# Weighted rows of an attention layer as two float32r parts, a ring of 10 groups instead of 12, and a later change of the scatter lag

## The reference

```
# first layer: an MLP on each edge, its mean at the source node
h = concat([x[src], x[dst]]);  h = tanh(h @ W0 + b0);  h = tanh(h @ W1 + b1)
h = (h @ W2 + b2) * (edge_attr @ Wg)
x = layernorm(x + segment_mean(h, src))
# second layer: attention with 4 heads of 64
h = einsum('ni,hio->hno', x, W);  e = leaky(attn_src[src] + attn_dst[dst]) * edge_weight
alpha = exp(e - max(e)) / segment_sum(exp(e - max(e)), dst)
x = layernorm(x + segment_sum(h[src] * alpha, dst))
```

## Time and profile before

| | us |
|---|---|
| median of 3 runs | 2397.0 |
| lowest and highest | 2392.29, 2398.76 |
| profiled execution | 2396.2 |
| its span, first to last instruction | 2394.1 |

### The profile page before, as it was taken

How to read it: one execution, slowest core, us unless ns; L and a number is a source line. 1 busy time by engine, 2 the same in 40 slices (tenths; PEclk the granted TensorE clock), 3 DMA queues, 4 the chain that set the end, 5 groups by cost and what they waited for, 6 DMA issues and landing times. The chain is left out here.

```text
span 2394.1 us, 38204 instructions
## 1 busy us (share of the span) xinstructions
PE 1902.2 (79%) x12132; PEld 1623.5 (68%) x12132; DVE 1426.5 (60%) x4037; ACT 1211.2 (51%) x2298; POOL 1522.9 (64%) x1253
## 2 busy tenths in 40 slices
PE   7799999989999999999999999954245555455560
PEld 7688888878888888888888888843133444333350
DVE  6556666656666666666666666653165455454475
ACT  2477777757777777777777777734000000000012
POOL 0427777777787777777777777734655565555513
PEclk9899999999999999999999999977566676766685
DMA  7798877777777777777777887674344444444423
GB/s 247 253 237 198 179 169 163 153 152 157 163 163 161 161 165 160 164 163 162 163 162 169 175 177 174 134 198 122 97 110 121 120 131 118 119 114 122 114 80 110
DMA packets 239706, 370.92 MB, mean 155 GB/s; under 512 B 33255, under 2 KB 172481, under 8 KB 239495
## 3 DMA queue, kind: packets, MB, share of 16 engines
q0 software_dynamic: 104688, 191.38, 40.5%
q1 hardware_dynamic: 134807, 177.00, 25.0%
HBM read 260.28 MB, written 107.97 MB: 154 GB/s over the span
## 5 line engine op out<-in xcount | busy, mean ns | idle before, releaser
L1549 POOL DMA_INDIRECT accA<-ystage,to_a x391 | 639.3, 1635 | 204.7 <-issue 105.7
L1555 POOL DMA_INDIRECT GA<-TA,src_c x391 | 436.5, 1116 | 246.0 <-issue 108.5
L1606 POOL DMA_INDIRECT Hg<-HT,src_c x391 | 376.2, 962 | 266.9 <-DVE xb L1118 152.0
L644 DVE TENSOR_TENSOR h2l<-h2f,h2h 128x512 fp32r<-128x512 f32 (+1 forms) x294 | 203.2, 691 | 307.3 <-ACT h2h L1997 159.9
L1681 PE MATMUL bank<-h1h,W1h 128*128 128x512 f32 x882 | 355.1, 403 | 12.9 <-DVE h1l L644 12.9
L1682 PE MATMUL bank<-h1l,W1h 128*128 128x512 f32 x882 | 349.0, 396 | 0.0
L1683 PE MATMUL bank<-h1h,W1l 128*128 128x512 f32 x882 | 348.8, 395 | 0.0
L2034 ACT ACTIVATE h1f<-bank 128x512 f32<-128x512 f32 (+1 forms) x392 | 220.7, 591 | 243.0 <-PE bank L1736 196.8
L1926 PE MATMUL bank<-xb,in_window 128*128 128x260 f32 (+1 forms) x782 | 277.3, 501 | 62.5 <-issue 60.7
L2177 ACT ACTIVATE drop<-neg_m 128x1 f32<-128x1 f32 x49 | 14.4, 295 | 548.9 <-DVE neg_m L1113 376.5
L1926 PEld LDWEIGHTS bank<-xb,in_window 128*128 128x128 f32 (+1 forms) x782 | 187.9, 252 | 112.7 <-issue 82.2
(11 more groups left out here) (252 smaller groups left out, 4498.3 us busy)
## 6 DMA issues: line engine op xcount, KB each, us to landing
ef<-in_eT SPq DMA_DIRECT2D x97, 256.0 KB
bcast_i<-in_src_row SPq DMA_DIRECT2D x97, 256.0 KB
TW<-TB SPq DMA_DIRECT2D x116, 203.0 KB
HB<-hist SPq DMA_DIRECT2D x98, 130.0 KB
rel<-RL SPq DMA_DIRECT2D x97, 128.0 KB
rem<-RD SPq DMA_DIRECT2D x48, 256.0 KB
TB<-stB SPq DMA_DIRECT2D x24, 406.0 KB
accA<-zeros SPq DMA_DIRECT2D x4, 2193.0 KB, 15.6
```

The source lines that it names most:

```text
L644: return dve.tensor_tensor(o, full, hi.bitcast(f32), ALU.subtract)
L1549: return pool.indirect_dma_start(out=table, out_offset=bass.IndirectOffsetOnAxis(ap=rows, axis=0), in_=sums, in_offset=None, compute_op=AL ...
L1555: pool.indirect_dma_start(out=GA[0:n, b % (GAR * BLOCKS_PER_GROUP), :].bitcast(f32), out_offset=None, in_=TA, in_offset=bass.IndirectOffse ...
L1606: pool.indirect_dma_start(out=Hg[0:n, slot, :], out_offset=None, in_=HT, in_offset=bass.IndirectOffsetOnAxis(ap=src_c[0:n, b:b + 1], axis= ...
```

## The change

It does five things.

1. `SLOW_START` goes from 20 to 91: `lag` is 3 for groups 0 to 90.
2. `HGR` goes from 12 to 10, and `chosen`, used after the last pair, lies in slots of `Hg`.
3. `xb` becomes a plain float32 ring of 2 groups without the weights' columns. ACT copies it into `xb_hi` (float32r, 4 groups; new `upper_rows`), whose last 4 columns are the exponentials; DVE subtracts `xb_hi` from `xb` into `xb_lo` (float32r, 2 groups; new `lower_rows`), once a group, and once a pair the 4 weight columns. `in_window` becomes float32r.
4. `window_sums` does two float32r products a block, one with `xb_hi` and one with `xb_lo`, and waits for `s_xb_lo` rather than `s_xb`.
5. The semaphores `s_pad` and `s_mg` are merged into `s_zero` and `s_nm`, with the counts changed to suit; the other branch gets a buffer of its own, `xb_u`.

`lower_rows(2q)` stands on DVE after `weighted_rows(2q + 1)`, and `lower_rows(2q + 1)` after `edge_scores(q + 2)`, ahead of `one_hot(q + 3)`. `same_rows` splits a list of blocks into those with 128 rows and the last, shorter one; `lo(o, full, hi)` is a DVE subtraction.

```diff
-SLOW_START = 20
+SLOW_START = 91
...
-        chosen = sb("chosen", [P, NT, NG], f32, sc)
...
-        HGR = 12
+        HGR = 10
...
+        chosen = Hg[:, 2 * BLOCKS_PER_GROUP:HGR * BLOCKS_PER_GROUP, :].rearrange("p b d -> p (b d)")[:, 0:NT * NG]\
+            .rearrange("p (t g) -> p t g", g=NG)
...
-        xb = sb("xb", [P, XBR * BLOCKS_PER_GROUP, BW], f32, s2)
-        in_window = sb("in_window", [P, XBR * BLOCKS_PER_GROUP, P], f32, s2)
+        xb = sb("xb", [P, 2 * BLOCKS_PER_GROUP, OUT], f32, s2)
+        xb_hi = sb("xb_hi", [P, XBR * BLOCKS_PER_GROUP, BW], f32r, s2)
+        xb_lo = sb("xb_lo", [P, 2 * BLOCKS_PER_GROUP, BW], f32r, s2)
+        xb_u = sb("xb_u", [P, BW], f32, s2)
+        in_window = sb("in_window", [P, XBR * BLOCKS_PER_GROUP, P], f32r, s2)
...
             def weighted_rows(g):
 
                 dve.wait_ge(s_ex, g // 2 + 1)
+                if g >= 2:
+                    dve.wait_ge(s_xb_lo, g - 1)
+                for run in same_rows(blocks_of_group(g)):
+                    n, b, k = rows_of_block(run[0]), run[0], len(run)
+                    i, r = b % (2 * BLOCKS_PER_GROUP), b % (HGR * BLOCKS_PER_GROUP)
+                    last = weigh(xb[0:n, i:i + k, :], Hg[0:n, r:r + k, 0:OUT], weight_p(g // 2)[0:n, i:i + k], n, k)
+                last.then_inc(s_xb, 1)
+
+            def lower_rows(g):
+
+                if g % 2 == 0:
+                    dve.wait_ge(s_S, g)
+                    for run in same_rows(blocks_of_window_pair(g // 2)):
+                        n, b, k = rows_of_block(run[0]), run[0], len(run)
+                        j, i = b % (XBR * BLOCKS_PER_GROUP), b % (2 * BLOCKS_PER_GROUP)
+                        lo(xb_lo[0:n, i:i + k, OUT:BW], weight_p(g // 2)[0:n, i:i + k], xb_hi[0:n, j:j + k, OUT:BW])
+                dve.wait_ge(s_xb_hi, g + 1)
                 for run in same_rows(blocks_of_group(g)):
                     n, b, k = rows_of_block(run[0]), run[0], len(run)
                     j, i = b % (XBR * BLOCKS_PER_GROUP), b % (2 * BLOCKS_PER_GROUP)
-                    r = b % (HGR * BLOCKS_PER_GROUP)
-                    last = weigh(xb[0:n, j:j + k, 0:OUT], Hg[0:n, r:r + k, 0:OUT], weight_p(g // 2)[0:n, i:i + k], n, k)
-                last.then_inc(s_xb, 1)
+                    last = lo(xb_lo[0:n, i:i + k, 0:OUT], xb[0:n, i:i + k, :], xb_hi[0:n, j:j + k, 0:OUT])
+                last.then_inc(s_xb_lo, 1)
 
             def carry_window(g):
 
...
                     weighted_rows(2 * q + 1)
+                    lower_rows(2 * q)
                 if 0 <= q - 1:
...
                     edge_scores(q + 2)
+                if 0 <= q < NQ:
+                    lower_rows(2 * q + 1)
                 if q + 3 < NQ:
...
             def window_sums(g):
 
                 pe.wait_ge(s_win, g // 2 + 1)
-                pe.wait_ge(s_xb, g + 1)
+                pe.wait_ge(s_xb_lo, g + 1)
                 if g >= 3:
                     pe.wait_ge(s_carry, g - 2)
                 blocks = blocks_of_group(g)
                 for b in blocks:
                     n, j = rows_of_block(b), b % (XBR * BLOCKS_PER_GROUP)
-                    last = pe.matmul(PS[g % 3][:, 0:BW], in_window[0:n, j, :], xb[0:n, j, :],
-                                     start=b == blocks[0], stop=b == blocks[-1])
+                    pe.matmul(PS[g % 3][:, 0:BW], in_window[0:n, j, :], xb_hi[0:n, j, :], start=b == blocks[0], stop=False)
+                    last = pe.matmul(PS[g % 3][:, 0:BW], in_window[0:n, j, :], xb_lo[0:n, b % (2 * BLOCKS_PER_GROUP), :],
+                                     start=False, stop=b == blocks[-1])
                 last.then_inc(s_S, 1)
 
             pe.wait_ge(s_hc, NT)
...
 
 
             act.wait_ge(s_dc, DC["no maximum"])
-            for q in range(NQ):
-                act.wait_ge(s_nm, q + 1)
+            def exponentials(q):
+
+                act.wait_ge(s_nm, 2 * (q + 1))
                 act.activation(drop[:, q:q + 1], neg_m[:, q:q + 1], ACT.Exp, bias=neg_m[:, q + 1:q + 2], scale=-1.0)\
                     .then_inc(s_drop, 1)
                 if q >= 2:
...
                     j, i = b % (XBR * BLOCKS_PER_GROUP), b % (2 * BLOCKS_PER_GROUP)
                     act.activation(weight_p(q)[0:n, i:i + k], score[0:n, b:b + k, :], ACT.Exp,
                                    bias=neg_m[0:n, q + 1:q + 2])
-                    last = act.activation(xb[0:n, j:j + k, OUT:BW], score[0:n, b:b + k, :], ACT.Exp,
+                    last = act.activation(xb_hi[0:n, j:j + k, OUT:BW], score[0:n, b:b + k, :], ACT.Exp,
                                           bias=neg_m[0:n, q + 1:q + 2])
                 last.then_inc(s_ex, 1)
+
+            def upper_rows(g):
+
+                act.wait_ge(s_xb, g + 1)
+                if g >= XBR:
+                    act.wait_ge(s_S, g - XBR + 1)
+                for run in same_rows(blocks_of_group(g)):
+                    n, b, k = rows_of_block(run[0]), run[0], len(run)
+                    j, i = b % (XBR * BLOCKS_PER_GROUP), b % (2 * BLOCKS_PER_GROUP)
+                    last = copy(xb_hi[0:n, j:j + k, 0:OUT], xb[0:n, i:i + k, :])
+                last.then_inc(s_xb_hi, 1)
+
+            exponentials(0)
+            for q in range(NQ):
+                upper_rows(2 * q)
+                if q + 1 < NQ:
+                    exponentials(q + 1)
+                upper_rows(2 * q + 1)
             for i in range(2):
                 last = act.activation(factor[:, :].rearrange("p (q i) -> p q i", i=2)[:, :, i], neg_m[:, 1:NQ + 1], ACT.Exp,
                                       bias=neg_m[:, NQ:NQ + 1], scale=-1.0)
```

More of the change, by code:

```diff
@@ L492, in build_program @@
         s_sp = sem("s_sp")
-        s_mg = sem("s_mg")
         s_nm = sem("s_nm")
@@ L499, in build_program @@
         s_xb = sem("s_xb")
+        s_xb_hi = sem("s_xb_hi")
+        s_xb_lo = sem("s_xb_lo")
         s_S = sem("s_S")
@@ L1107, in running_maximum @@
                 if q >= 2:
[L1108 to L1112, removed]
+                    dve.wait_ge(s_nm, 2 * (q - 1))
+                dve.tensor_reduce(top_g[:, q % 2:q % 2 + 1], PTOP[:, 0:P], AX.X, ALU.max).then_inc(s_nm, 1)
+                dve.wait_ge(s_nm, 2 * q + 1)
                 dve.scalar_tensor_tensor(neg_m[:, q + 1:q + 2], top_g[:, q % 2:q % 2 + 1], -1.0, neg_m[:, q:q + 1],
@@ L1288, in _ @@
                     dve.wait_ge(s_vg, 64 * NB + 16 * (b + 1))
-                    step(dve.tensor_copy(xb[0:n, 0, OUT:BW], score[0:n, b, :]))
-                    step(weigh(xb[0:n, 0:1, 0:OUT], Hg[0:n, 0:1, 0:OUT], score[0:n, b:b + 1, :], n, 1), ("weighed", b))
+                    step(dve.tensor_copy(xb_u[0:n, OUT:BW], score[0:n, b, :]))
+                    step(weigh(xb_u[0:n, 0:OUT].unsqueeze(1), Hg[0:n, 0:1, 0:OUT], score[0:n, b:b + 1, :], n, 1), ("weighed", b))
             def attention_residual(c):
@@ L1358, in _ @@
             sp.dma_start(TB[N:N + P, :].rearrange("p (k d) -> p k d", k=4),
-                         zeros[:, 0:H0 // 2].unsqueeze(1).to_broadcast([P, 4, H0 // 2])).then_inc(s_pad, 16)
+                         zeros[:, 0:H0 // 2].unsqueeze(1).to_broadcast([P, 4, H0 // 2])).then_inc(s_zero, 16)
             sp.wait_ge(s_dc, DC["rem"])
@@ L1428, in _ @@
                         sp.wait_ge(s_tb[k], stores(N0R, k))
-                    sp.wait_ge(s_pad, 16)
+                    sp.wait_ge(s_zero, 16)
                 if g + 2 < NG:
@@ L1580, in _ @@
                 if 0 in added:
-                    pool.wait_ge(s_zero, 32 * TABLES)
+                    pool.wait_ge(s_zero, 16 + 32 * TABLES)
                 for j in range(BLOCKS_PER_GROUP):
@@ L1913, in spread_maxima @@
                 if q >= 1:
-                    pe.wait_ge(s_mg, q)
+                    pe.wait_ge(s_nm, 2 * q - 1)
                 pe.matmul(PTOP[:, 0:P], ones[:, :], diag[:, q % 2, :], start=True, stop=True).then_inc(s_sp, 1)
@@ L1980, in _ @@
                         pe.wait_ge(s_vact, VACT1 + 1 + b)
-                    pe.matmul(bank[0][0:n, 0:BW], in_window[0:n, 0, 0:n], xb[0:n, 0, :],
+                    pe.matmul(bank[0][0:n, 0:BW], in_window[0:n, 0, 0:n].bitcast(f32), xb_u[0:n, :],
                               start=True, stop=True).then_inc(s_vpe, 1)
```

1 line of the change is left out of this document (removed).

## The result

The changed kernel takes 2371.6 us in the median of 5 runs (2358.39 to 2381.24) against 2397.82 for the kernel before: ratio 0.9881, 95% interval 0.985 to 0.9913. It is 26 us faster where 25 us slower was forecast. The forecast had POOL's waits for `xb` at 180 to 190 us and the remote wait near 200; they came out at 93.1 and 116.6. The profiled execution has a span of 2356.3 us and a mean TensorE clock of 0.849.

A forecast was written before the change was run, and what follows sets the result against it. It took PE to bound most of the first layer, and POOL's gathers, pausing for credits while PE's results came late, the second. Terms 26 + 4 - 2 + 6 - 8 = +26 us gave 2422; own range 2402 to 2458, overall 2300 to 2462.

The forecast's parts named there:

- A rule against the change: Second layer: DVE subtractions with two SBUF inputs contend with POOL's gathers; +10 us for 3 of 16, +60 for all.
- rival C: Second layer: subtractions beside gather runs cost +89 us at most, 2511, or give 2432 to 2482; 0.14 together with Rival B.
- Step 1: Second layer, split on DVE and ACT: odd group's subtraction lengthens POOL's pause from 7.1 to 8.4 us; +26 (0 to +55).
- Step 2: Second layer, ring of 10 groups: 48 instead of 56 gathers run free; +4 us (0 to 8.4), 2 taken off.
- Step 3: Second layer after the last gather: one pair less in the ring, five pairs pay 2.63 us each; +6 (0 to 13).
- Step 4: Second layer's window products: float32r makes them shorter, but nobody waits for PE's work, only for its results; 0.
- rival A: Second layer: float32r brings PE's results sooner, the remote wait goes; 2246 in full (chance 0.11), 2331 in part (0.21).
- Step 6: First layer, the longer lag: PE's loss at 458 to 551 goes, SP's tile wait returns later; -8 us (-19 to +5).
- Rival B: Second layer: late credits cut POOL's runs to 12 gathers; 2481, or 2451 with only the even subtraction; 0.14 with rival C.
- Rival D: Whole kernel: the lag's full -19 us pays for the split at half price; 2398, no change; chance 0.09.

The follow-up runs named there:

- lower_psum: Changed kernel with DVE's large subtraction replaced by an equally long product with one PSUM input, PE multiplying xb_hi twice: 2420.62 against 2390.54 us, ratio 1.0105.
- split_f32_2: Changed kernel with one float32 product of xb_hi a block, xb_lo made but not multiplied, on a chip holding results back: 2388.29 us, ratio 0.9992.
- ring10: Kernel before with HGR 10 instead of 12 and nothing else, on a chip not holding results back: 2201.02 us, ratio 0.9997.
- upper_only: Changed kernel without lower_rows: DVE subtracts nothing, PE multiplies xb_hi twice; results held back: 2382.28 us, ratio 0.9975.
- after_lag20: Changed kernel with SLOW_START back at 20, on a chip not holding results back: 2226.44 us, ratio 1.0095 to the kernel before.
- lag_only: Kernel before with only SLOW_START changed from 20 to 91, on a chip not holding results back: 2198.75 against 2204.75 us, ratio 0.9978.
- type_only_2: Kernel before with two float32r products a block, both of the same rows, no split; results held back: 2398.29 us, ratio 1.0048.
- after_paced3: Changed kernel with POOL also waiting for L1906 of the pair 3 before; results not held back: 2215.5 against 2203.58 us, ratio 1.0058.
- few_ad: Kernel before with one instead of three products per block in destination_scores; results not held back: 2204.29 us, ratio 1.0002.
- Paced: Kernel before with SLOW_START 91 and POOL waiting before each pair's gathers for PE's L1906 of the pair 4 before: 2317.2 us, ratio 0.9696.
- paced3: Kernel before with SLOW_START 91 and POOL waiting for PE's L1906 of the pair 3 before: 2313.0 us, ratio 0.9667; repeated, 2314.85 us, 0.9703.
- gap: Kernel before with SLOW_START 91 and a 0.43 us POOL copy once in every four gathers: 2351.72 us, ratio 0.9815.

## Why the prediction was wrong

*The step that failed* is the one on the port ("A rule against the change"), with its rival C. The sum has no term for the port, and C priced the stall of a gather beside a subtraction as a cost only, +10 to +89. Its size is now seen: the gathers took 24.8 us more in all (1.026 for 0.962 in the mean). The +89 supposes 73 gathers held for a whole subtraction of 1.22; no run shows that, and in after 36 gathers took over 1.2 us. The mark of C, a mean over 1.00 us, came, but the price had the wrong sign. I had myself written that PE's results are held while gathers are issued without a gap, and that pauses make it good; a stall is such a gap, and I didn't put the two sentences together. On the chips that hold results back the gaps bring more than they cost: without them the change is at 1.0105 (lower_psum), with them at 0.9881 to 0.9929, a difference of 1.8 to 2.2%, some 42 to 54 us, between different sets of runs; on one chip split_f32_2 is 32 us under lower_psum. The Trainium skill ("SBUF — State Buffer", the section "Who interferes with whom") says that a VectorE instruction contends with a GpSimd instruction that reads SBUF when it has two SBUF inputs. The runs agree: with one input in PSUM (lower_psum) the gathers' mean is 0.954, with both in SBUF 1.022 to 1.038 where results are held back and 0.989 to 0.995 where they are not.

*Step 1, the pause longer by the odd subtraction:* right without the stalls. lower_psum is what I had forecast, 2422 with waits for `xb` of 180 to 190: 2420.62 and 185.7. By its parts, against the first profile of before: 31.6 more from the first gather to the end of the last (672.4 to 640.8; steps 1 and 2 had 28), and half a us less in the tail, where step 3 had +6. So part of the agreement of the totals is luck. The durations were right too: 1.22 for the subtraction and 1.06 for the copy, 1.22 and 1.1 forecast.

```profile
L648 DVE TENSOR_TENSOR xb_lo<-xb,xb_hi 128x1024 fp32r<-128x1024 f32 x97 | 118.0, 1216 | 0.0
...
L2019 ACT ACTIVATE xb_hi<-xb 128x1024 fp32r<-128x1024 f32 x97 | 102.5, 1057 | 466.6 <-DVE xb L1120 370.8 <-issue 57.6 <-PE bank L1948 38.2
```

*Step 2, the ring:* nothing in ring10, on a chip where there was nothing to cost. Its price where results are held back wasn't measured alone; upper_only, with the ring, the lag, the copy and the lighter products, is 0.25% under before.

*Step 3, the tail:* on the first chip it did not grow. It is 1.4 us shorter, with three scores behind the last gather where five stood before: two pairs fewer, not one, and each pair 2.4 us dearer. On the chip of after_lag20 it is 6.8 us longer than in lag_only, with one score behind the last gather in both. That this is near the +6 is luck; the term was made from five pairs.

*Step 4, the type:* 0 by itself, as taken (1.0001 and 1.0048). Beside the gaps it seems to be worth up to 1% (split_f32_2 against after on other chips), which I hadn't seen and no run shows by itself. The mark of *rival A* came in the first profile, waits for `xb` under 100 (93.1; 110.0 and 117.2 in the two later runs of after), but A's cause did not: type_only_2 has 149.0.

*Step 6, the lag:* right in each part that was measured. 6.0 and 4.2 us where -8 was taken, both on chips that don't hold results back, and 7.4 by the first gather of the profile. The windows answer to the earlier trace rows: PE is busy through 458 to 551, and in the second layer its clock is lower, 0.55 for 0.69.

```profile
458.00:551.00 93.00, 93.00 (x610) 81.52 (x610) 62.33 (x197) 70.10 (x127) 74.57 (x54) 1.00 0.78 164
...
2000.00:2100.00 100.00, 40.56 (x334) 36.39 (x332) 69.05 (x135) 22.67 (x40) 64.25 (x65) 0.55 0.47 128
```

SP's wait for the tile is now at the layer's end, 20.5 us more than the 30.0 that stood in the same stretch before, 16 to 23 forecast:

```profile
SPq L577 <- DMA accA<-spill,spill_i: 50.5, 2, 30.2
```

*Rival B* did not come: in after most runs of gathers still have 16 or 8, none has 12, and the pauses sum to less, not more. *Rival D* needed 19 us from the lag, which is worth 4 to 7.

*What I could not have known:* that the hold, the base of all of steps 1 to 3, is there on some chips and not on others. With it the change is 0.7 to 1.2% faster. Without it it is slower: 0.95% with the old lag (after_lag20), 0.6% with after's lag and a wait that never stops POOL (after_paced3).

*Open:* what holds PE's results back, whether it depends on their number (few_ad met the wrong kind of chip), and how a gap of 0.4 to 0.6 us shortens the hold, since in the first profile of after most of the held waits end some 15 us after the last stall began. Paced, paced3 and gap show that breaking up the gathers pays, and lower_psum that the place of the input decides over the stalls; the way from the stall to the earlier result is argued.

## What to carry to other kernels

When the profile shows results that arrive only once another engine's stream of DMA issues stops, look first at who else breaks that stream, and price each stall of it with both signs: what it costs the stream, and what it may give back by ending a hold sooner. Such a stream is better stopped on purpose, by a wait for the late result itself (0.967 to 0.970 here), than by a side effect of other work. And a gain of 1% that hangs on such a hold should be measured on more than one chip before it is kept: here it was 0.7 to 1.2% faster on some chips and, as far as after_paced3 tells it, 0.6% slower on another.

## What was not expected of the hardware

- One and the same kernel took 2388 to 2398 us in four sets of runs and 2204 in two, on other chips, 8% apart. Most of the difference is in the second layer's 391 gathers, 640.8 us with pauses (before, the first profile) and 494 without (lag_only).
- DVE's subtraction of 128x1024 with both inputs in SBUF made a gather that began inside it last longer by what was left of it less 0.13 us: 1.58 us for one that began 0.48 into it (2085.72), 1.93 for one that began 0.12 into it (2246.92), instead of 0.96. In after's trace this holds within 0.02 us for all 59 gathers that began inside one with 0.2 us or more left. Those that began before it and ran into it, 77, all took 0.96 or less: only the start of a gather is held. Together the lengthened ones account for all of the 24.8 us.
- Adding 98 operations of 0.43 us to POOL, the engine that issued all gathers, made the kernel 39 us faster (the lag's 4 to 7 us included).
